# A spline stage in another order: down units first, class units last, on one core of a fused two-layer block

## The reference, cut to what matters

```
def spline_reconstruct(control_points, out_size, in_size):
    n = out_size * in_size
    idx, f = _catmull_rom_grid(control_points.shape[0], n)
    p0, p1, p2, p3 = (control_points[idx[0]], ..., control_points[idx[3]])
    f2 = f * f; f3 = f2 * f
    w = 0.5 * (2*p1 + (p2-p0)*f + (2*p0-5*p1+4*p2-p3)*f2 + (3*p1-p0-3*p2+p3)*f3)
    return w.reshape(out_size, in_size)
gate_w = spline_reconstruct(gate_cp, 2048, 512)     # up_w alike
down_w = spline_reconstruct(down_cp, 512, 2048)
# feed-forward on the layernormed x:  (silu(xn @ gate_w.T) * (xn @ up_w.T)) @ down_w.T
```

## Time and profile before

| what | us |
|---|---|
| runs, median of 3 | 1543.31 |
| profiled execution, its own time | 1553.67 |
| span of the profiled execution | 1551.9 |
| TensorE busy, whole span | 1305.2 |
| VectorE busy, whole span | 1156.8 |
| ScalarE busy, whole span | 660.5 |
| GpSimd busy, whole span | 468.5 |
| spline stage, from first to last instruction | 291.3 to 363.6 |
| first TensorE instruction of feed-forward 0 | 364.05 |

### The profile page before, as it was taken

One profiled execution on the slowest core, in us unless ns is written; L12 is line 12 of the kernel. 1 busy time (PEld: TensorE's weight loads), 2 busy tenths in 40 slices (PEclk: granted clock), 3 DMA queues, 4 the chain that ended last, 5 costly groups with the idle time before them and its releaser, 6 DMA issues. The chain is left out here.

```text
span 1551.9 us, 20163 instructions
## 1 busy us (share of the span) xinstructions
PE 1305.2 (84%) x7496; PEld 655.0 (42%) x7496; DVE 1156.8 (75%) x1527; ACT 660.5 (43%) x1047; POOL 468.5 (30%) x343
## 2 busy tenths in 40 slices
PE   5499998267798979885387888779999999999996
PEld 3278777222343434442022222234444454444443
DVE  5567778757688767994477767588888888888865
ACT  3445664356344444433254635234333334333322
POOL 0032432245555566641276597400000000000000
PEclk8789998567899999997598989999999999999999
DMA  8412231247233241225001103130000000000000
GB/s 299 136 59 66 83 109 58 76 141 231 80 112 129 99 136 68 82 95 190 27 1 43 26 14 94 56 122 8 7 7 14 7 7 7 7 7 14 7 8 14
DMA packets 59590, 106.51 MB, mean 69 GB/s; under 512 B 10863, under 2 KB 21767, under 8 KB 59388
## 3 DMA queue, kind: packets, MB, share of 16 engines
q1 hardware_dynamic: 58236, 101.34, 19.9%
q0 software_dynamic: 1280, 4.20, 0.9%
HBM read 73.47 MB, written 27.66 MB: 65 GB/s over the span
## 5 line engine op out<-in xcount | busy, mean ns | idle before, releaser
L1682 PE MATMUL FD<-W0D,HH 128*128 128x512 f16 x512 | 159.3, 394 | 11.7 <-DVE HM L1740 9.2
L2533 PE MATMUL HD<-W1H,HT 128*128 128x512 f16 x512 | 154.9, 379 | 0.0
L2336 DVE TENSOR_REDUCE NQ<-A_M 128x2 f32<-128x1024 f32 x60 | 73.3, 1222 | 54.3 <-PE A_M L2183 54.1
L1676 PE MATMUL FG<-F,W0G 97*128 97x512 f16 x324 | 84.7, 393 | 25.3 <-PEq L1043 8.7
L2479 ACT CAST OS<-SS 128x2048 f16<-128x2048 f32 x16 | 30.4, 1898 | 169.9 <-DVEq L2607 169.9
L335 ACT ACTIVATE DD<-E,TM 128x128 f32<-128x128 f32 x256 | 72.7, 370 | 68.7 <-PE E L431 67.1
L1607 POOL TENSOR_TENSOR HL<-HM,HH 128x512 f16<-128x512 f32 x48 | 76.0, 1584 | 84.9 <-ACT HH L1636 84.9
L1682 PE MATMUL FD<-W0D,HL 128*128 128x512 f16 x256 | 100.0, 391 | 0.0
L2533 PE MATMUL HD<-W1L,HT 128*128 128x512 f16 x256 | 97.0, 379 | 0.0
L2136 ACT ACTIVATE PT<-A_S,CM 128x1024 f32<-128x1024 f32 x64 | 70.9, 1111 | 58.8 <-PE A_S L2209 58.7
L2585 DVE SCALAR_TENSOR_TENSOR H<-HU,DS,SG 128x512 f32<-128x512 f32 x64 | 48.0, 751 | 61.7 <-ACT SG L2468 57.3
(11 more groups left out here) (368 smaller groups left out, 3033.8 us busy)
## 6 DMA issues: line engine op xcount, KB each, us to landing
VALP<-in_ffn_weights_dram SPq DMA_DIRECT2D x24, 512.0 KB, 3.9
VALQ<-in_ffn_weights_dram SPq DMA_DIRECT2D x24, 512.0 KB
quantised_weights<-QQ SPq DMA_DIRECT2D x24, 512.0 KB, 2.7
X<-in_x_dram SPq DMA_DIRECT2D x8, 1024.0 KB, 6.1
W1H<-quantised_weights SPq DMA_DIRECT2D x3, 2048.0 KB, 8.1
F<-features_kept SPq DMA_DIRECT2D x16, 288.0 KB
CTX<-in_ctx_dram SPq DMA_DIRECT2D x4, 1024.0 KB, 6.9
features_kept<-XQ SPq DMA_DIRECT2D x4, 1024.0 KB, 7.0
```

The costliest lines, as they stand in the source:

```text
L1676: last = pe.matmul(banks[t][:, :], GW[rows, t, lhs, cols], F[b % 2][rows, rhs, c, :], start=(n == 0), stop=(n == 2))
L1682: last = pe.matmul(DN[c][:, :], lhs[:, at, c * P:(c + 1) * P], W2[:, i, part, :], start=(i == 0 and n == 0), stop=(i == KI - 1 and n == 2))
L2336: v.tensor_reduce(NQ[:, i % NC, at:at + 2], first_bank(g, i)[:, :, :], AX.X, ALU.max, negate=True).then_inc(mx_taken, 1)
L2533: ins = pe.matmul(DN[:, :], HT[:, q, lp, k, :], W[:, 2, i * D:(i + 1) * D], start=(i == 0 and lp == 0 and W is WH), stop=(i == KI - 1 and ...
```

## The change

The 24 units and the 8 chunks (two to a turn) become 28 **turns** of the one ring of bank pairs. Turns 0, 1, 4 and 7 are chunk turns; down units take the other turns up to 19, class units turns 20 to 27. The features are spread: one transposes group k a turn (turns 4 to 7 for batch 0, 16 to 19 for batch 1), half a moments group a turn (turns 10 to 13, 22 to 25), single normalised tiles and statistics between. `quantiser.scales` moves to VectorE's beginning, right after the first statistics. On SyncE the powers table and RH come first, each RH quarter with its own semaphore; the class tables come after; the stores of the down weights are issued between batch 0's transfers (k = 0 and 4) and after them (8 and 12); XQ and MQ of batch 1 and their reloads come last. The feed-forward 0 code only calls the split helpers with all their parts, in the old order.

```diff
+CHUNK_TURNS = (0, 1, 4, 7)
+TURNS = UNITS_W + CHUNKS // 2
+TURN_X = {4: (0, 0), 5: (0, 1), 6: (0, 2), 7: (0, 3), 16: (1, 0), 17: (1, 1), 18: (1, 2), 19: (1, 3)}
+MOMENT_X = {10: (0, 0, 0), 11: (0, 0, 1), 12: (0, 1, 0), 13: (0, 1, 1), 22: (1, 0, 0), 23: (1, 0, 1), 24: (1, 1, 0), 25: (1, 1, 1)}
+NORM_X = {1: ((0, 0), (0, 1)), 2: ((0, 2), (0, 3)), 12: ((1, 0),), 13: ((1, 1),), 14: ((1, 2),), 15: ((1, 3),)}
+STATS_X = {5: 4, 6: 5, 8: 6, 9: 7, 14: 8, 15: 9, 16: 10, 17: 11, 18: 12, 19: 13, 20: 14, 21: 15}
+SPREAD_X = {0: (0, NC), 11: (NC, 2 * NC), 23: (2 * NC, TILES)}
...
@@ sync @@
+            sp.dma_start(PW[:, :], A["spline_powers"]).then_inc(pw_loaded, 16)
             for q in range(RUNS // QW):
...
+            features.load(sp)
+            sp.dma_start(SEL..., A["class_select"]...).then_inc(loaded, 16)
+            sp.dma_start(MKC[:, :], A["class_second"]).then_inc(loaded, 16)
+            sp.dma_start(IDX[:, :], A["class_rows"]).then_inc(idx_loaded, 16)
...
             features.keep_elements(sp, 0)
+            keep_down(0)
             features.near_elements(sp, 0)
+            keep_down(4)
             features.keep_moments(sp, 0)
             features.near_moments(sp, 0)
+            keep_down(8)
+            keep_down(12)
+            features.keep_elements(sp, 1)
+            features.near_elements(sp, 1)
+            features.keep_moments(sp, 1)
+            features.near_moments(sp, 1)
@@ tensor @@
+            for n in range(TURNS):
+                if n in TURN_X:
+                    b, k = TURN_X[n]
+                    features.transposes(pe, b, [k], T)
+                if n in MOMENT_X:
...
+                    features.moments(pe, b, m, range(2 * part, 2 * part + 2), T)
+                if n >= 3:
+                    chunks = sum(m <= n - 3 for m in CHUNK_TURNS)
+                    if n - 3 in CHUNK_TURNS:
+                        pe.wait_ge(emptied, chunks)
+                    else:
+                        pe.wait_ge(wf_selected, n - 2 - chunks)
...
@@ Features.transposes @@
         pe.wait_ge(self.xn_ready, b * NC + NC)
+        alone = len(ks) == 1
+        if not alone or ks[0] < 2:
+            self.t_free(pe)
+        else:
+            pe.wait_ge(self.xl_ready, b * KD + ks[0] - 1)
```

More of the change, by code:

```diff
@@ L1084, in high @@
                 nc.scalar.copy(weights(u, 0), WF[0:rows(u), u % 4, :]).then_inc(wh_ready, 1)
+            u = 0
             act.wait_ge(eps_ready, 1)
[L1087 to L1110, removed]
-                        act.wait_ge(features.xq_kept, 16)
-                    features.high(act, 1, range(2 * half, 2 * half + 2), T)
-                if u == MOMENT_UNIT_1:
-                    act.wait_ge(features.mq_kept, 16)
-                    features.high_moments(act, 1, T)
+            for n in range(TURNS):
+                act.wait_ge(filled, n + 1)
+                if n in CHUNK_TURNS:
+                    act.wait_ge(ct_zero, 1)
+                    for half in range(2):
+                        j, t, g = chunk(n, half)
+                        nc.scalar.copy(CT[CT_HIGH:CT_HIGH + PIECES * POLY, t, g * SUB:(g + 1) * SUB],
+                                       banks(n)[half][0:PIECES * POLY, :]).then_inc(ct_high, 1)
+                else:
+                    if u >= 4:
+                        act.wait_ge(wl_ready, u - 3)
+                    nc.scalar.copy(WF[0:rows(u), u % 4, :], banks(n)[0][0:rows(u), :]).then_inc(wf_copied, 1)
+                    if u:
+                        high(u - 1)
+                    u += 1
+                if n in SPREAD_X:
+                    first, end = SPREAD_X[n]
+                    act.wait_ge(mv_ready, end)
+                    nc.scalar.activation(SD[:, first:end], MV[:, first:end, 1], ACT.Sqrt, bias=EPS[:, 0:1]).then_inc(sd_ready, 1)
+                if n in TURN_X:
+                    b, k = TURN_X[n]
+                    if b and k == 0:
+                        act.wait_ge(features.xq_kept, 16)
+                    features.high(act, b, [k], T)
+                if n in MOMENT_X:
+                    b, m, part = MOMENT_X[n]
+                    if part:
+                        if b and m == 0:
+                            act.wait_ge(features.mq_kept, 16)
+                        features.high_moments(act, b, [m], T)
@@ L1164, in _, with spread @@
             v.memset(EPS[:, :], 1e-5).then_inc(eps_ready, 1)
+            n_eps = 1
+            def spread(m):
+                first, end = SPREAD_X[m]
+                v.wait_ge(st_ready, end)
+                for n in range(first, end):
+                    v.bn_aggr(MV[:, n, :], ST[:, n, :]).then_inc(mv_ready, 1)
             for n in range(NC):
                 v.bn_stats(ST[:, n, :], X[:, n, :]).then_inc(st_ready, 1)
-            v.wait_ge(st_ready, NC)
-            for n in range(NC):
-                v.bn_aggr(MV[:, n, :], ST[:, n, :]).then_inc(mv_ready, 1)
```

271 lines of the change are left out of this document (131 added, 140 removed).

## The result

The kernel after takes 1552.25 us (median of 20 runs, 1546.61 to 1561.6), the kernel before beside it 1544.24 (20 runs, 1538.26 to 1552.07). The ratio is 1.004, with a 95% interval of 1.0022 to 1.0057: slower by about 6 us (the two medians are 8.0 apart, near the interval's upper end). The forecast was 1540.9, range 1533 to 1549, with 0.49 for no change and 0.17 for slower. It missed.

The account below looks back on a forecast made before the run. SyncE's queue, not an engine, was taken to end the spline stage. Stage +0.3 and feed-forward 0 -2.7 sum to -2.4 us, from the runs' median 1543.31 to 1540.9 us, range 1533 to 1549.

Parts of the forecast that it names:

- +0.3 for the stage: End of the spline stage: TensorE starts feed-forward 0 at 363.0 to 365.7, middle 364.4, or +0.3 us.
- -2.7 for the start of feed-forward 0: Start of feed-forward 0: an earlier gather saves part of 7.1 us of unexplained waits, middle of -5.5 and 0.
- SyncE's queue ends the stage: End of the spline stage: SyncE's chain of stores, landings and reloads, not an engine, sets it; TensorE starts 0.45 us later.
- The milestones to the normalised batch 0: Start of the stage: statistics, scales, chunks, norms and unit 0's selection were to give batch 0 normalised at 304.3.
- turns 16 to 19 in 10.8: Batch 1's feature turns: its `low` ends 10.8 us after its norms, two pairs 9.0 and first fill 1.8.
- the XQ store held behind `keep_down(12)`: SyncE's queue: batch 1's XQ store waits for unit 15's low part and goes out at 343.2 to 346.0.
- SyncE's tail of 19.75: From batch 1's XQ store to TensorE's start of feed-forward 0: two landings, reloads and hand-over, together 19.75 us.
- RH's first quarter: Load for the first down unit, costed at nothing; rival: landing after 11.3 us costs +5.5, 1546.4 us, chance 0.08.
- slow clock at the end: Rival for turns 22 to 25: turns of 3.6 instead of 1.9 us, stage +6.8, 1547.4 or 1550.1 us, chance 0.12.
- its term between the last down fill and the XQ store: Before batch 1's XQ store: class matmuls 1.92, 0.2, copy and cast 1.15, GpSimd 1.16, leading to 342.7 to 345.4.
- on the fast clock VectorE paces and batch 1 is normalised at 330.0; on the slow clock at 332.7: Turns 8 to 15: VectorE at about 1.5 us a turn paces on the fast clock; moment matmuls cost 0.43 or 0.21 each.
- down products under 28 us after the start: Feed-forward 0: down products starting under 28 us after the stage begins, before 34.4, were to show the forecast wrong.

Follow-up runs that it names:

- experiment 0: The kernel before, profiled once more with no edit: one execution of 1543.72 us, stage 72.0 us.
- experiments 1: Changed kernel with the reload of batch 1's moments moved to the head of feed-forward 0's SyncE queue: ratio to the kernel before 1.0018, stage 70.4 us.
- 2: Kernel before with the reload of batch 1's moments moved to the head of feed-forward 0's SyncE queue: ratio 0.9963, on a repeat 0.9986.
- experiment 4: Changed kernel with batch 1's XQ store queued ahead of the last store of down weights: ratio to the kernel before 1.0015, stage 75.7 us.
- Experiment 9: Changed kernel without the products of XQ's low parts in batch 0's moments, 8 matmuls instead of 16: ratio to the kernel before 1.0031, stage 75.3 us.
- experiment 3: Changed kernel with each down unit's two matmuls issued twice in turns 5 to 15: ratio to the kernel before 1.0046, stage 81.5 us.
- experiment 8: Changed kernel with chunks in turns 0 to 3, class units before down units, SyncE's old queue order but powers loaded earlier: ratio to the kernel before 0.9995.
- 10: Changed kernel with the features' transposes in pairs again, in turns 5, 7, 17 and 19: ratio to the kernel before 1.0051, stage 77.3 us.
- experiment 12: Changed kernel with four added products of class rows ahead of each down fill in turns 8 to 13: ratio to the kernel before 1.0066, stage 83.9 us.
- experiment 13: Changed kernel with two added products of XQ ahead of each down fill in turns 10 to 13: ratio to the kernel before 1.0001, stage 80.5 us.

## Why the prediction was wrong

The forecast's sum was +0.3 for the stage and -2.7 for the start of feed-forward 0. The stage gave +5.0 (+5.7 against experiment 0), and the second term nothing. By medians the change cost +8.0 where -2.4 was forecast, 10.4 us apart: 5.4 of them are the stage (5.7 against 0.3), 2.7 the second term. The 2.3 us that are left have the size of the 2.65 by which the stage starts later in the profiles, and their cause is open.

**Right.** The clue that SyncE's queue ends the stage: experiments 1, 2 and 4. The milestones to the normalised batch 0 (304.3 forecast, 304.9 measured, with 1.2 of it from the later start), the 2.8 us wait at turn 4 (2.87), `low` of k = 3 at 318.4 (319.5), turns 16 to 19 in 10.8 (11.1), the XQ store held behind `keep_down(12)` (2.4 forecast, 1.9 measured), SyncE's tail of 19.75 (20.4). The class units hide under the landings. RH's first quarter was in time: TensorE's first down fill, at 299.19, waited 3.10 us for its mask, but VectorE worked on without a gap until 305.6. The clock did come up in turns 22 to 25, so the rival "slow clock at the end" did not occur.

**Right by luck, or mis-sized without effect.** A class unit is four matmuls, not the eight that the description of the kernel before gives: the 32 matmuls of line 1150 in the trace of before fill eight units, and after the change two units take 1.94 us (at 345.46) and one 1.06. The forecast took the 1.92 of eight matmuls for one unit. So its term between the last down fill and the XQ store is about 1 us too long, which helped to cover the turns that were too short, and its rival of a slow clock at the end was priced about 1 us a turn too high. The class moments with their 11.3 us were issued behind the powers too (292.04), not right behind the mask. And the lower bound of 1537.5 should have been 1536.7 by the forecast's own terms (-1.1 and -5.5).

**Wrong, turns 8 to 15.** The step "on the fast clock VectorE paces and batch 1 is normalised at 330.0; on the slow clock at 332.7" put the slow clock's price on the moments alone and laid them beside VectorE's turns. VectorE's own work was sized well (12.10 us busy). But in the trace TensorE paces the four turns with moments: 1.86 for a quarter of the moments and 0.92 for the down fill in series, 2.78 a turn, where the forecast had about 1.5 to 1.8, and VectorE's 5.2 us of waiting come on top of its work. The stretch took 17.3, not 11.6 to 14.3. Experiment 9 (8 matmuls fewer, 3.8 us less) and experiment 3 (more fills, 4.1 us more) show it. Against the middle of the forecast (norms 40.0 us after TensorE's first instruction, measured 44.3; stage 73.0, measured 77.7) this is 4.3 us of the stage's miss of 4.7. The rest, to rounding: turns 16 to 19 +0.3, the held store -0.5, the tail +0.7.

**Wrong, the start of feed-forward 0.** The step "I take the middle, -2.7" gave half a chance to a cause that is not there. The 7 us appear in three of the sixteen profiled executions: the first of before, and experiments 1 and 8, which have the gather early and late. All others, the kernel before among them, have the down products 26.2 to 27.4 us after the start. In those three the waits fall 14 to 21 us after the gather's first issue, but other gathers pass without any. What sets them off stays open. The forecast had named down products under 28 us after the start as a sign of being wrong, and they came at 27.0. A term read off one execution, with no producer behind it, should have been priced at nothing with its own small chance.

**Why the order costs.** Experiments 8 and 10 divide it. The spreading of the transposes: nothing. The order of the units, with its chunk turns and queue: 3.7 us. In turns 8 to 15 it is 3.1, with the clock at 0.74 against 0.50; what else experiment 8 gains up to XQ's store it largely gives back in its longer tail. A part of the 3.7 is the queue: experiment 4, which keeps the new order and only takes away what held the XQ store, is at 75.7, 1.7 over experiment 8. The ring of turns with chunks in it, against the kernel before, at most 2.0 (74.0 against 72.0); only argued, since no run had the old chunks with the new order.

Three rows of VectorE in the kernel before show where its XQ of batch 1 was ahead: batch 0's last `low`, batch 1's last norms, batch 1's last `low`.

```profile
307.84 1.29 DVE L1517 SCALAR_TENSOR_TENSOR XQ<-ST,XQ 128x512 f16<-128x512 f32 x2
...
325.05 0.98 DVE L1506 TENSOR_SCALAR XN<-X,MV,RS 128x512 f32<-128x512 f32 x2
...
336.71 1.29 DVE L1517 SCALAR_TENSOR_TENSOR XQ<-ST,XQ 128x512 f16<-128x512 f32 x2 [0.29 <-ACT XQ L1512]
```

From TensorE's first instruction to batch 0's XQ it is 17.8 us before and 27.0 after; from there to the norms of batch 1 it is 16.9 and 17.3; from there to batch 1's XQ 12.0 and 11.1. So against the kernel before the delay of 8.7 us arises ahead of turn 8, where scales, chunks and the first down units now stand among batch 0's features. The forecast had these 27.0 us right. It missed because it gave 11.6 to 14.3 to the stretch behind them, for which the kernel before had needed 16.9 with the same sixteen moments and four norms. The trace of before would have shown the doubtful term. The gains that the order offered, no stores in SyncE's tail and a gather that starts with the stage, were worth little: in all profiles shown here the first down products wait for HM, not for the gather. The rise of XQ's completion from 46.6 us after the start to 55.4 is what SyncE's 20 us of landings turned into time; the stores gone from the tail took 3.7 of these 8.7 us back (26.1 from XQ's completion to TensorE's start before, 22.4 after).

## What to carry to other kernels

Behind a result that leaves the chip's engines and comes back through two serial landings, what delays its completion is paid for in large part (3.3 and 3.8 us earlier gave 2.4 each), and what fits under the landings costs nothing: place that result first, then ask what the landings hide, and move a reload that the next stage needs late into that stage. When engines take turns, add up each engine's own turn at the slow clock before saying who paces, and hold the sum against what the same work took in the trace before. Profile the kernel before twice before a wait without a producer is put into a sum.

## What the runs showed of the hardware beyond that

TensorE stood without a gap from 319.6 to 332.5 at a granted clock of 0.50 (1.2 GHz). With added products of 84 or 128 rows it did so for 20 and 16 us (experiments 12 and 13), and with the doubled fills of 24 rows for 27 us (experiment 3, 312.06 to 338.98, mean clock 0.51). With the class units first a quarter of the moments fell from 1.87 to 1.03 us at about 320.5, in the same turns, and the clock stayed up beside the down fills that followed.

In every profile of the turns the moments that began beside class products alone were at the fast clock by their third or fourth quarter, at the stage's end of the changed kernel too. Quarters of the moments that began beside down fills of 24 rows never rose to it, not even with class products added (experiment 12). But in the kernel before all sixteen moments in one row, between down fills too, brought it up (mean clock 0.59 over the 5.99 us from 338.14). The fills ahead of them and behind them:

```profile
334.01 2.74 PE L1158 MATMUL SP<-W0D,PWB 24*128 24x512 bf16 x6
...
344.06 1.46 PE L1158 MATMUL SP<-W0D,PWB 24*128 24x512 bf16 x6
```

So down fills put between the moments go with the slow clock here, and the same fills around them do not keep it down. No run took only the fills out of these turns with the rest kept, so it is open whether they decide it.

In experiment 13, 2.8 us more in this stage came with 7.4 us less behind it, at a higher clock in parts of feed-forward 0.
